# Softmax row sums in a fused attention and feed-forward layer: turned by VectorE and sent through DRAM instead of through TensorE

## The reference, cut to what matters

```python
scores = jnp.einsum('bhqd,bhkd->bhqk', q, k) / math.sqrt(Hd)
scores = scores + causal[None, None]
attn = jax.nn.softmax(scores, axis=-1)
out = jnp.einsum('bhqk,bhkd->bhqd', attn, v)
...
x = _layernorm(x + _L0_attn_ref(x, L0_attn_w_qkv, L0_attn_b_qkv, L0_attn_w_out, L0_attn_b_out), axis=-1)
x = _layernorm(x + _L0_ffn_ref(x, L0_ffn_gate_w, L0_ffn_gate_scale, L0_ffn_up_w, L0_ffn_up_scale, L0_ffn_down_w, L0_ffn_down_scale), axis=-1)
```

## Time and profile before

| | before |
|---|---|
| median of 3 runs | 734.27 us (732.36 to 735.01) |
| profiled execution | 732.33 us, span 730.5 us |
| PE busy | 711.2 us (97%) |
| DVE, ACT, POOL busy | 386.0, 373.1, 187.0 us |
| instructions | 11735 |

### The profile page before, as it was taken

How to read it: one execution, slowest core, us unless ns; L and a number is a source line. 1 busy time by engine, 2 the same in 40 slices (tenths; PEclk the granted TensorE clock), 3 DMA queues, 4 the chain that set the end, 5 groups by cost and what they waited for, 6 DMA issues and landing times.

```text
span 730.5 us, 11735 instructions
## 1 busy us (share of the span) xinstructions
PE 711.2 (97%) x4368; PEld 551.7 (76%) x4368; DVE 386.0 (53%) x988; ACT 373.1 (51%) x900; POOL 187.0 (26%) x198
## 2 busy tenths in 40 slices
PE   7999899999999999999999999999999999999994
PEld 6777577777777677776688888888888888888883
DVE  4766576666667665577552322553344533544335
ACT  3676676767776776777765653322232222322230
POOL 0011610347132660418833233221020002000004
PEclk9999999999999999999999999999999999999998
DMA  9821453346741577314688964852321013000111
GB/s 306 222 79 30 87 135 126 87 98 143 204 135 59 123 168 235 75 39 116 154 179 162 209 148 145 219 193 79 144 70 45 0 43 129 0 1 1 57 59 59
DMA packets 97207, 83.35 MB, mean 114 GB/s; under 512 B 64128, under 2 KB 73344, under 8 KB 97024
## 3 DMA queue, kind: packets, MB, share of 16 engines
q1 hardware_dynamic: 90624, 62.69, 30.8%
q0 software_dynamic: 6528, 19.93, 12.1%
HBM read 59.53 MB, written 22.02 MB: 112 GB/s over the span
## 4 chain that ended last, share of the span: by engine, by line
PE 92%; POOL 4%; DVE 2%; issue 1%; DMA 1%; ACT 0%; POOLq 0%; SPq 0%; DVEq 0%
PE bank L1506 16%; PE bank L1507 16%; PE bank L1293 12%; PE bank L1372 9%; PE bank L1514 7%; PE bank L1513 7%; PE bank L1311 6%; PE bank L1355 5%; PE bank L1330 5%; PE bank L1393 5%; POOL z_tok L684 1%; PE bank L1404 1%; PE bank L1259 1%; POOL xT_lo L717 1%; DVE probs L1048 1%; POOL z_tok L810 1%
## 5 line engine op out<-in xcount | busy, mean ns | idle before, releaser
L840 ACT ACTIVATE probs<-probs,neg_max 128x128 f32<-128x128 f32 (+3 forms) x256 | 140.3, 552 | 3.0 <-DVE neg_max L1048 2.9
L1048 DVE CUSTOM_DVE_ANT_0 probs<-bank,causal 128x128 f32<-128x128 f32 (+3 forms) x256 | 111.7, 484 | 41.2 <-PE bank L1355 41.2
L1166 DVE SCALAR_TENSOR_TENSOR hid<-bank,u_scale,silu 128x512 f32<-128x512 f32 x64 | 48.0, 750 | 157.2 <-PE bank L1507 156.0
L1506 PE MATMUL bank<-xT_hi,gateT 128*128 128x512 f32 x256 | 99.7, 389 | 0.0
L1507 PE MATMUL bank<-xT_lo,gateT 128*128 128x512 f32 x256 | 99.6, 389 | 0.0
L1506 PE MATMUL bank<-xT_hi,upT 128*128 128x512 f32 x256 | 99.6, 389 | 0.0
L1507 PE MATMUL bank<-xT_lo,upT 128*128 128x512 f32 x256 | 99.6, 389 | 0.0
L1372 PEld LDWEIGHTS bank<-ident,probs 128*128 128x128 f32 x640 | 71.5, 140 | 35.0 <-issue 24.2
L948 ACT ACTIVATE silu<-bank,g_scale 128x512 f32<-128x512 f32 x64 | 44.0, 688 | 102.2 <-PE bank L1507 102.2
L898 ACT ACTIVATE probsT<-bank 128x512 f32<-128x512 f32 x80 | 47.7, 596 | 92.0 <-PE bank L1372 90.1
L954 ACT ACTIVATE hid_hi<-hid 128x512 fp32r<-128x512 f32 x58 | 36.7, 632 | 107.7 <-DVE hid L1166 107.7
(11 more groups left out here) (105 smaller groups left out, 1164.0 us busy)
## 6 DMA issues: line engine op xcount, KB each, us to landing
halves<-x_tok SPq DMA_DIRECT2D x7, 1024.0 KB, 6.4
x_tok<-halves SPq DMA_DIRECT2D x7, 1024.0 KB, 8.2
scan_buf<-in_L_ffn_gate_w_dram SPq DMA_DIRECT2D x4, 1024.0 KB, 6.1
scan_buf<-in_L_ffn_up_w_dram SPq DMA_DIRECT2D x4, 1024.0 KB, 5.4
scan_buf<-in_L_ffn_down_w_dram SPq DMA_DIRECT2D x4, 1024.0 KB, 5.3
w_int<-in_L_ffn_gate_w_dram POOLq DMA_DIRECT2D x16, 256.0 KB, 3.0
w_int<-in_L_ffn_up_w_dram POOLq DMA_DIRECT2D x16, 256.0 KB, 3.2
w_int<-in_L_ffn_down_w_dram POOLq DMA_DIRECT2D x16, 256.0 KB, 4.0
```

The source lines that it names most:

```text
L840: nc.scalar.activation(probs[qb][:, j, :], probs[qb][:, j, :], ACT.Exp, bias=neg_max[:, qb, j:j + 1], scale=-1.0, accum_out=row_sum[:, qb, ...
L1048: nc.vector.tensor_tensor_reduce(out=probs[qb][:, j, :], in0=score[j][:, first:first + w], in1=causal[:, S - w:S], scale=-SCALE, scalar=-F ...
L1166: nc.vector.scalar_tensor_tensor(out=hid[:, i % 2, :], in0=bank[:, :], scalar=u_scale[:, i:i + 1], in1=silu[:, i % 2, :], op0=ALU.mult, op ...
L1506: nc.tensor.matmul(acc[n][:, :], w[:, c, cols], form(xT_hi[:, c, :]), start=c == 0, stop=False)
```

## The change

TensorE, GpSimd and ScalarE no longer touch the inverse row sums. VectorE writes them in the order head, block into the first 4 columns of each of four 8-column parts of a 128x32 tile, and turns that tile in 32x32 blocks (`turn_inverse`, at step 8 right behind the second `inverse_sum`, which moves there from step 9; at step 2 in the last group). A DMA stores the turned tile in DRAM (16 KB, in pieces of 128 bytes); a second, which waits for the first, reads the 4 x 512 values back, each head's row to 32 partitions (`inv_rows`, 256 KB). `normalise` waits for it and multiplies `pv_acc` by `inv_rows`. SP issues both, except in the last group, where ScalarE does, at its steps 2 and 6.

```diff
-    INVERSE_STEP = 15
+    TURN = 32
+    STORE_STEP, SPREAD_STEP = 2, 6
...
+        def store_inverse(eng, G):
+            eng.wait_ge(inv_turned_done, G + 1)
+            eng.dma_start(inv_dram.rearrange("j (q a r) -> (j q) a r", a=P // TURN, r=TURN).rearrange("c a r -> a c r"),
+                          inv_turned[:, :]).then_inc(inv_stored, 16)
+
+        def load_inverse(eng, G):
+            eng.wait_ge(inv_stored, 16 * (G + 1))
+            if G > 0:
+                eng.wait_ge(normed, G)
+            eng.dma_start(inv_rows[:, :], inv_dram[:, 0:S].unsqueeze(1).broadcast_to((HG, HD, S))).then_inc(inv_spread, 16)
...
-                if G in SCAN_GROUPS[1:]:
+                if G in SCAN_GROUPS[1:] and g != 3:
                     load_scan(SCAN_GROUPS.index(G))
...
                 if g == 2:
-                    turn(b + 2)
+                    if b == LAST:
+                        turn(b + 2)
+                    spread_inverse(G)
+                    if G + 1 in SCAN_GROUPS:
+                        load_scan(SCAN_GROUPS.index(G + 1))
+                    if b < LAST:
+                        turn(b + 2)
...
                 if g == 3:
                     store_halves(b + 2)
+                if g != 2 and G < GROUPS - 1:
+                    spread_inverse(G)
...
-                widen_inverse(G)
...
+                    if s == STORE_STEP and G == GROUPS - 1:
+                        store_inverse(act, G)
+                    if s == SPREAD_STEP and G == GROUPS - 1:
+                        load_inverse(act, G)
...
-                    if s == INVERSE_STEP:
-                        keep_inverse(G)
...
-                nc.vector.reciprocal(inv_sum[:, qbs, :], row_sum[:, qbs, :]).then_inc(inv_done, 1)
+                nc.vector.reciprocal(inv_sum[:, :, qbs].rearrange("p j q -> p q j"), row_sum[:, qbs, :]).then_inc(inv_done, 1)
+
+            def turn_inverse(G):
+                if G > 0:
+                    dve.wait_ge(inv_stored, 16 * G)
+                wait_alone(dve, inv_done, 2 * (G + 1))
+                nc.vector.transpose(inv_turned[:, :], inv_sum[:, :, :].rearrange("p j q -> p (j q)")).then_inc(inv_turned_done, 1)
...
-                wait_drained(dve, "r", G)
+                dve.wait_ge(inv_spread, 16 * (G + 1))
+                if G > 0:
+                    dve.wait_ge(att_ready, G)
                 dve.wait_ge(pv_full, G + 1)
-                nc.vector.tensor_tensor(attT[:, :], pv_acc[:, :], attT[:, :], ALU.mult).then_inc(normed, 1)
+                nc.vector.tensor_tensor(attT[:, :], pv_acc[:, :], inv_rows[:, :], ALU.mult).then_inc(normed, 1)
...
-                    if s == 9:
+                    if s == (8 if G < GROUPS - 1 else 2):
                         inverse_sum(G, 1)
+                        turn_inverse(G)
```

More of the change, by code:

```diff
@@ L201, in postln_block_kernel @@
                 banks.whole(("w", W_STEPS[G, s]))
-            if s == INVERSE_STEP:
-                banks.whole(("r", G))
             banks.part(jobs, sum(counts[:s]), counts[s])
@@ L218, in postln_block_kernel @@
     halves_dram = [None] + [nc.dram_tensor(f"halves{n}", (2 * D, S), U16, kind="Internal").ap() for n in range(1, 2 * B)]
+    inv_dram = nc.dram_tensor("inverses", (HG, TURN // HG * P), F32, kind="Internal").ap()
     x_v = x.rearrange("b (t p) d -> b p t d", p=P)
@@ L316, in postln_block_kernel @@
         row_sum = sb("row_sum", [P, NT, HG], F32, att)
[L317 to L319 removed]
+        inv_sum = sb("inv_sum", [P, HG, TURN // HG], F32, att)
+        inv_turned = sb("inv_turned", [P, TURN], F32, att)
+        inv_rows = sb("inv_rows", [P, S], F32, att)
         attT = sb("attT", [P, S], F32, att)
@@ L1397, in weighted_values @@
                     last.then_inc(pv_full, 1)
-            def transpose_inverse(G):
-                acc = bank_for("r", G)
-                pe.wait_ge(inv_widened, G + 1)
-                for qb in range(NT):
-                    last = nc.tensor.transpose(acc[:, qb * P:(qb + 1) * P],
-                                               inv_wide[:, qb, :, :].rearrange("p j d -> p (j d)"), ident[:, :])
-                last.then_inc(full_of("r", G), 1)
             transpose_x(0)
@@ L1453, in _ @@
                         transpose_weights(W_STEPS[G, s])
-                    if s == INVERSE_STEP:
-                        last_products = products_at(STEPS) if G == GROUPS - 1 else []
-                        for m in last_products[:-1]:
-                            weighted_values(G, m)
-                        transpose_inverse(G)
-                        for m in last_products[-1:]:
+                    if s == STEPS - 1 and G == GROUPS - 1:
+                        for m in products_at(STEPS):
                             weighted_values(G, m)
```

23 lines of the change are left out of this document (8 added, 15 removed).

## The result

| | before | after |
|---|---|---|
| median | 734.64 us (732.36 to 735.49, 4 runs) | 747.04 us (744.73 to 750.27, 4 runs) |
| ratio | | 1.016, 95% interval 1.012 to 1.020 |
| profiled span | 730.5 us | 744.9 us |

A forecast was written before the change was run, and what follows sets the result against it. TensorE alone was taken to bound attention, except group 14, where the chain runs through GpSimd. -7.1 + 3.2 + 1.3 + 1.0 = -1.6 us gave 732.7 us against the 734.27 median, with an 8-in-10 range of 727.7 to 739.5.

The forecast's parts named there:

- What goes: Inverses' transposes off TensorE's chain: 6.2 us in groups 0 to 13, 0.3 in 14, 0.59 in 15; together 7.1.
- VectorE's turning: One 128x32 turning per group on VectorE, taken as 0.3 us, costing nothing outside group 14.
- Ordinary groups hidden: Store, load and issuing take 7.1 us, at worst 10.5, of 11.8 available before the product, so cost nothing.
- Groups 7 and 11: Store behind other work in SP's queue; product 4.0 us late, 2.4 free: 1.6 each, 3.2 together, ends 0 and 11.
- the 1.0 that was added for a clash: Groups 7 and 11: GpSimd's weight DMA, some 7 us earlier, among transposes and y1 stores; lateness 3.0 becomes 4.0.
- the whole stretch only shifts with the groups: Groups 7 and 11: times of before were used, shorter groups only shifting the stretch; no lateness counted for it.
- Group 3 hidden: Group 3 has no y1 stores, and `turn` goes out after group 2's inverses while TensorE waits for input: no cost.
- Group 14 to 15: ScalarE's copies of probabilities late behind its own store and load in group 15: 1.3 us, ends 0.2 and 4.0.
- the layer's start: Feed-forward layer: `d_scale` 2.9 us late behind SP's store and load, 2.0 free: cost 1.0, ends 0 and 2.5.
- B: SP's queue in groups 7 and 11: product 7.9 us late, 5.5 lost in each; 740.5 us, chance 0.15.
- C: Narrow load on four DMA engines: 1.4 us more per crossing, 1.2 in the last group; 736.7 us, chance 0.12.
- A: All covered: load lands in 2 to 3 us, nothing else late beyond the free 2.4; 727.7 us, chance 0.27.

The follow-up runs named there:

- f4: Changed kernel without the inverses' store and load (product takes another tile, no wait), and SP's eight transposes (`turn`) at their old place: 730.8 us.
- f3: Changed kernel, but GpSimd issues its 512 KB weight DMA only after the group's second reciprocal, as before the change: 750.9 us.
- e5: Changed kernel, but the load of the inverses reads its rows from eight places in DRAM instead of four: 739.6 us.
- e3: Changed kernel with both DMAs issued, but the product multiplies by the value bias and VectorE doesn't wait for them: 744.4 us.
- f1: Changed kernel with `turn` back at its old place ahead of the inverses, and the next group's scan load behind them: 738.1 us.
- e2: Changed kernel with neither DMA of the inverses issued; the product takes the value bias and nothing waits: 732.8 us.
- h1: Changed kernel with `turn` at its old place except in group 2, and group 15's store and load issued by GpSimd: 734.8 us.
- e1: Changed kernel, but in groups 3, 7 and 11 SP issues the inverses' pair ahead of y1 stores, residual and halves: 749.6 us.

## Why the prediction was wrong

The spans differ by +14.4 us where the sum had -1.6. Of the 16.0 between them 8.4 are in the two crossings, 6.3 in the last groups and the layer, 0.9 in groups 0 and 1 and 0.4 in the crossing into group 4.

1. **What goes** (-7.1): right per group, 0.43 to 0.45 against 0.44, and 1.0 in groups 14 and 15 against 0.9 (f4). Only groups 0 and 1 gave nothing: group 2 starts at 66.00 in both kernels.
2. **VectorE's turning** (0.3): 0.21 us, as near the reciprocal's 0.20 as was thought.
3. **Ordinary groups hidden**: right; the load is issued 1.97 after the store there, and VectorE waits for `inv_rows` four times in all, in groups 4, 8, 12 and 15.
4. **Groups 7 and 11** (3.2 us) is the step that failed; 11.6 was lost there against the new group length. The order of events was right, the lateness 6.8 instead of 4.0, or of 3.0 before the 1.0 that was added for a clash. The inverses' store landed 1.2 later than in the sum: its transposes took 14.1 us to issue instead of 10.9 (how much of this is the clash, f3 can't tell), and a shorter wait for the y1 stores and quicker halves took 2.0 back. The load took 1.7 more (5.7 instead of 4.0, since it is narrow, by e5). And 0.9 is a term that was put at nothing: "the whole stretch only shifts with the groups" holds for SP's queue, which starts from group 6, but the product's place moves up by two shorter groups against it. 3.0 + 1.2 + 1.7 + 0.9 = 6.8. The low clock after the idle time added 1.6 to each. And the step asked only who waits for the product: behind SP's wait for the store stood the scan load, which costs 5.0 and 4.2 of the 5.8 when nobody waits for the product (e3). So even a product in time would have gained 0.8 and 1.6.
5. **Group 3 hidden**: the new place of `turn` in group 2 was rightly seen as harmless; the old one would cost 6 us (f1). The crossing into group 4 lost 0.4 (67.4 against 67.0 in e2), not nothing: VectorE waited 1.5 us for `inv_rows` there.
6. **Group 14 to 15** (1.3) and **the layer's start** (1.0), 2.3 together against 7.4 + 0.3 + the lost gain of 0.9: mis-sized by more than three. The first place was right, ScalarE's copies late behind its own store. That store took 5.95 us, not 2.5; the upper end for this place was named (5) and not taken. The clock added over 2 us here too. The second did not show: the layer itself came 7.4 us later, so its first `silu` waited for TensorE and not for `d_scale`. The thin cover is real, though, and shows where TensorE comes in time: 3.2 us of wait in f4, 4.62 in h1.
7. **Rivals.** B, SP's queue, had the right mechanism for the product and 7.9 late against 6.8, with 740.5 us; it had neither the scan load nor the lower clock. C was true as to the width. They were set as alternatives, but both held at once, with the last groups on top. A held in the ordinary groups only.

## What to carry to other kernels

A store and a load that depends on it, put into an in-order queue, make everything behind the wait late, so list for each item behind it who waits, before asking when the pair itself lands: here the scan load alone cost nearly as much as both together. When a stretch of the queue is already full, take the upper ends for transfers in it, and add rivals that share a cause instead of choosing between them. The same trick was worth 0.8% once the pair was left out where the queue is full and nothing covers it (groups 14 and 15) and each neighbour stood at the place that its own start allowed.

## What the runs showed of the hardware

- After 5 us with 1 us of work TensorE ran at 0.50 to 0.56 of its clock for some 3 us (16 score matmuls 1.66 us instead of 0.87). After 3.6 us without any, in group 15, it ran at 0.50 and 32 products took 3.14 instead of 1.65. In all, a stall of 4 to 5 us cost another 1.6 to over 2.
- A DMA that spreads 4 rows over 128 partitions keeps 0.20 to 0.26 of the sixteen DMA engines busy, with 8 rows of source 0.42 to 0.53. In the crossing that is 5.7 against 3.6 us.
- The same 16 KB store let its load go 1.97 us after its issue in a quiet group, 5.65 when a 512 KB DMA was issued 0.07 us before it (group 6 of f3), 8.1 behind 1 MB on its own queue.
- Four y1 stores of 256 KB landed 2.8 us after the last issue in the change as made, 6.6 with the inverses' load just in front of them (e1), 6.9 with a 512 KB DMA issued beside them (f3).
- Eight DMA transposes took 10.3 to 19.5 us to issue, depending on what else was in flight; the issue of an 8 KB load of scales in 4-byte pieces took 0.96 to 8.0 us.
